# Order of a few small VectorE and GpSimd steps at the seams between attention units

## The reference

```
x: 8 batches x 512 tokens x 128 channels;  16 heads of 64;  all float32
h = layernorm(x) * (1 + ca) + sa
q, k, v = h @ Wq.T, h @ Wk.T, h @ Wv.T          # each cut into 16 heads
q = q / |q| * q_scale ;  k = k / |k| * k_scale  # per head and token
p = softmax(q k^T / 8)                          # per head, 512 x 512
x = x + ga * (concat(p v) @ Wo.T + bo)
h = layernorm(x) * (1 + cb) + sb
x = x + gb * (experts(h) + shared(h))           # top 2 of 8 experts, GELU
```

## Time and profile before

| what | value |
|---|---|
| median of 3 runs | 1392.53 us (1389.64 to 1394.34) |
| profiled execution | 1390.22 us, of which the span is 1388.5 us |
| PE busy | 1252.9 us, 90% of the span |
| DVE busy | 1059.7 us, 76% |
| ACT busy | 977.0 us, 70% |
| POOL busy | 860.8 us, 62% |
| granted clock, mean | 0.973 of full speed |

### The profile page before, as it was taken

How to read it: one execution, slowest core, us unless ns; L and a number is a source line. 1 busy time by engine, 2 the same in 40 slices (tenths; PEclk the granted TensorE clock), 3 DMA queues, 4 the chain that set the end, 5 groups by cost and what they waited for, 6 DMA issues and landing times. The chain is left out here.

```text
span 1388.5 us, 31896 instructions
## 1 busy us (share of the span) xinstructions
PE 1252.9 (90%) x9674; PEld 818.7 (59%) x9674; DVE 1059.7 (76%) x1947; ACT 977.0 (70%) x2078; POOL 860.8 (62%) x1675
## 2 busy tenths in 40 slices
PE   4799999999999999999999999999995477999997
PEld 4555655656555565656565555666553355777775
DVE  3778877868777787778787777877773995788887
ACT  3677767777767776777777677777763564777776
POOL 2577667766667776677666677766746674444443
PEclk8899999999999999999999999999998798999999
DMA  5000000000000000000000000000002001434341
GB/s 133 1 2 1 2 1 2 2 4 2 1 4 2 2 1 4 2 2 2 4 2 2 4 2 2 2 2 2 1 2 77 0 0 26 122 90 101 89 94 32
DMA packets 53201, 28.60 MB, mean 21 GB/s; under 512 B 8720, under 2 KB 51224, under 8 KB 53016
## 3 DMA queue, kind: packets, MB, share of 16 engines
q1 hardware_dynamic: 51832, 25.99, 7.8%
q10 hardware_dynamic: 1184, 0.40, 0.1%
HBM read 24.16 MB, written 2.23 MB: 19 GB/s over the span
## 5 line engine op out<-in xcount | busy, mean ns | idle before, releaser
L714 ACT ACTIVATE probs<-bank,neg_max 128x512 f32<-128x512 f32 x512 | 347.2, 683 | 249.4 <-DVE neg_max L836 238.5
L836 DVE TENSOR_REDUCE neg_max<-bank 128x1 f32<-128x512 f32 x512 | 329.3, 685 | 161.0 <-PE bank L533 157.8
L573 PE MATMUL bank<-probsT,qkv 128*64 128x512 f32 x1024 | 276.2, 619 | 0.9 <-DVE oT L853 0.9
L533 PE MATMUL bank<-operands 64*128 64x512 f32 x1536 | 249.8, 430 | 1.4 <-ACT probs L714 0.9
L1003 POOL TENSOR_TENSOR inv_wide<-inv_sum,consts 128x512 f32<-128x512 f32 x64 | 66.5, 1039 | 220.9 <-DVE inv_sum L847 220.9
L549 PEld LDWEIGHTS T<-ident,probs 64*128 64x128 f32 x4096 | 170.0, 139 | 42.5 <-issue 14.7
L549 PE MATMUL T<-ident,probs 64*128 64x64 f32 x4096 | 171.1, 223 | 2.6 <-issue 1.4
L503 PEld LDWEIGHTS bank<-operands,hT_h 128*128 128x128 f32 x254 | 47.8, 188 | 209.7 <-issue 206.3
L1637 POOL TENSOR_TENSOR hid_l<-gated,hid_h 128x512 fp32r<-128x512 f32 x64 | 88.9, 1389 | 125.4 <-ACT hid_h L1554 125.4
L533 PEld LDWEIGHTS bank<-operands 64*128 64x128 f32 x1536 | 125.7, 186 | 63.3 <-issue 41.7
L842 DVE COPY probsT<-T 128x1024 f32<-128x1024 f32 x128 | 155.6, 1215 | 0.2
(11 more groups left out here) (237 smaller groups left out, 2379.2 us busy)
## 6 DMA issues: line engine op xcount, KB each, us to landing
probsT<-gate_scratch SPq DMA_DIRECT2D x64, 256.0 KB, 4.9
out<-x_all SPq DMA_DIRECT2D x8, 256.0 KB, 2.3
probsT<-in_L_ffn_fc_w SPq DMA_DIRECT2D x1, 1024.0 KB, 9.8
raw<-in_L_attn_Wq SPq DMA_DIRECT2D x1, 512.0 KB, 4.4
raw<-in_L_attn_Wk SPq DMA_DIRECT2D x1, 512.0 KB, 7.3
raw<-in_L_attn_Wv SPq DMA_DIRECT2D x1, 512.0 KB, 8.4
raw_o<-in_L_attn_Wo SPq DMA_DIRECT2D x1, 512.0 KB, 8.6
probsT<-in_L_ffn_sh_w SPq DMA_DIRECT2D x2, 256.0 KB, 2.7
```

The costliest lines, as they stand in the source:

```text
L533: last = nc.tensor.matmul(s_bank(hp, 2 * pair + head)[:], own[rows, q, toks], own[rows, k], start=((q, k) == (QH, KH)), stop=(q == QL))
L573: last = nc.tensor.matmul(O_BANK[rows, :], qkv[:, hp % 4, j, cols], probsT[:, hp % 2, head, j], start=(j == 0), stop=(j == NT - 1), skip_g ...
L714: nc.scalar.activation(probs[:, i % 4], s_bank(hp, i)[:], ACT.Exp, bias=neg_max[:, i:i + 1], accum_out=row_sum[:, hp % 2, i:i + 1]).then_i ...
L836: nc.vector.reduce_max(neg_max[:, i:i + 1], s_bank(hp, i)[:], AX.X, negate=True).then_inc(max_done, 1)
```

## The change

Two orders change, and no operation is added or removed.

On VectorE, in pair 0 of every slot, invert_sums(u-1) stands ahead of sum_squares(u+1) and guess_norms(u+1) instead of behind them. On GpSimd, in norm units, all four tiles of squares stand ahead of split_o(u-2); in the other units split_o stays between the first and the second tile.

```diff
@@ VectorE, slot
                             if pair == 2 and earlier >= 2:
                                 normalise(u - 2, hp - 2)
+                            if pair == 0 and earlier >= 1:
+                                invert_sums(u - 1, hp - 1)
                             if main and pair == 0 and with_next(b, hp, 1):
                                 sum_squares(u + 1)
                                 guess_norms(u + 1)
-                            if pair == 0 and earlier >= 1:
-                                invert_sums(u - 1, hp - 1)
@@ GpSimd, slot
                             square_projection(u + 2, hp + 2, 0)
-                        if earlier >= 2:
+                        split_late = main and norm_of(b, hp)
+                        if earlier >= 2 and not split_late:
                             split_o(u - 2, hp - 2)
                         if main and with_next(b, hp, 2):
                             for t in range(1, NT):
                                 square_projection(u + 2, hp + 2, t)
+                        if earlier >= 2 and split_late:
+                            split_o(u - 2, hp - 2)
```

## The result

The changed kernel takes 1360.16 us (median of four runs, 1358.57 to 1361.32) against 1393.01 us before; the ratio is 0.9767, with a 95% interval from 0.9747 to 0.9787. The gain is 32.9 us where 24 were forecast, and the time lies 0.8 us under the low end of the range. The direction and the places were right, the size was not.

A forecast was written before the change was run, and what follows sets the result against it. TensorE's waits in attention, behind the norm units, were taken as the bound. Seams and unit 3 in batches 1 to 6 (20.7 us), last batch 1.8, short slots 1.5: 24.0 us, bounds 21 and 31; median 1368.5 us, range 1361 to 1384.

The forecast's parts named there:

- the chain: Behind norm units: late GpSimd squares, then VectorE's sum and guess, inversion, widen, refinement; 1.75 us lost in unit 1, 3.03 in unit 4.
- the 5.25 us: Units 1 and 4: TensorE's third pair starts 5.25 us after the refinement, so an earlier refinement brings that pair forward.
- the entry wait of 0.40 us: Unit 3: VectorE stands 0.40 us for the last exponential before the inversion, which now goes ahead of the sum.
- the sum that starts 0.6 us later in unit 3: VectorE in unit 3: with the wait and the inversion ahead of it, the sum of squares is 0.60 us late.
- The rival on the slower side: Every slot: widen stretches the sum by up to 1.0 us, giving 1417 us; chance 0.06.
- the guess waits for widen: Seams at units 1 and 4: guess operations wait for a begun widen's end; the last starts 0.33 us after it.
- the shift from unit 3: Before unit 4: unit 3's refinement comes 0.49 us sooner, and layer norm's guess, inverse_std and squares come that much sooner.
- unit 3 loses 0.1 us: Unit 3: first exponential released at 465.03 against scores at 464.96, a loss of 0.1 us a batch.
- 4 x 0.3: Batch 0: second pairs wait less for the earlier refinement, up to 0.37 us, taken as 0.3 for each of four units.
- entry wait in every ordinary unit: Rival: 0.40 us comes through in 5 units of 8 batches, 16 us back, 1384.5 us; chance 0.12.
- blocked more than once: Rival: each of the guess's three operations may lose a turn to GpSimd, half the gain lost, 1380.5 us; chance 0.08.
- no change: Rival: the seams' wait passes to another engine and the refinement was not what counted, 1391 us; chance 0.04.

The follow-up runs named there:

- GpSimd's part alone: Against the kernel before, only GpSimd's new order: squares ahead of split_o in norm units, VectorE still sums first and inverts afterwards; 1371.16 us, ratio 0.9848.
- VectorE's part alone: Against the kernel before, only VectorE's new order: inversion ahead of the sum of squares, GpSimd keeps its old order in norm units; 1367.47 us, ratio 0.9824.
- widen kept back: Changed kernel with one wait more: widen starts only after the guess of the same slot, so not beside the sum; 1387.64 us, ratio 0.9966.
- the kernel with the short split_o: Against the kernel with statistics behind the maxima: split_o of norm units makes the low part for only 128 of 512 columns; 1358.08 us, ratio 0.9763.
- The second measurement: The changed kernel run again, unaltered, beside the kernel before on one chip; 1363.51 us, ratio 0.9778.

## Why the prediction was wrong

**What held.** The bound (TensorE's waits in two units of eight), the chain, the 5.25 us (in unit 4; 5.36 in unit 1), the entry wait of 0.40 us, and the sum that starts 0.6 us later in unit 3 (0.79 us ahead of the scores before, 0.18 after). What failed are sizes of terms in the sum, above all the refinement at unit 4 (forecast 2.70 us after the first scores, measured 2.23), and a term for TensorE's clock, which the sum doesn't have. They follow one by one. In unit 3 after, the inversion and the sum start as follows (VectorE's timeline), against the earlier trace rows:

```profile
449.97 0.20 DVE L847 RECIPROCAL inv_sum<-row_sum 128x8 f32<-128x8 f32 x1 [0.32 <-ACT probs L714]
450.17 1.22 DVE L813 TENSOR_REDUCE ss<-sq 128x16 f32<-128x1024 f32 x1
```

The wait is 0.32 us of idle time, as in the earlier trace rows. The sum beside widen was taken as unblocked, and it was: over all 64 units L813 takes 1.184 to 1.222 us after and 1.203 to 1.223 before. The rival on the slower side, and with it a stretched sum, is refuted. The Trainium skill gives tensor_reduce only the 1x mode, in "VectorE: DVE Perf Modes", "The perf-mode tier table (the rule you actually need)", as the prediction had it; these lengths, the same beside GpSimd and alone, agree.

**Step "the guess waits for widen" was oversized.** It added the whole 0.33 us from the sum's end to the last guess operation behind widen's end. But an operation that is blocked has already begun and ends with GpSimd's: L818 ended 0.04 us after widen, and the last guess operation started at 467.28, 0.15 us after it. That is 0.2 us too much at each seam. The step from there to the refinement, estimated at 0.27 us from no row of its own, took 0.25 (467.53 - 467.28). The prediction also put 0.1 us between split_o's end and widen at unit 4, where there is none (464.85 + 1.28 = 466.13, widen at 466.10). At unit 1 widen ended at 421.98 (420.94 + 1.04) and L818, at 421.83, was not held up at all:

```profile
420.94 1.04 POOL L1003 TENSOR_TENSOR inv_wide<-inv_sum,consts 128x512 f32<-128x512 f32 x1
...
421.83 0.18 DVE L818 TENSOR_SCALAR ss<-ss 128x16 f32<-128x16 f32 x1
```

**Step "the shift from unit 3" was undersized.** The squares of unit 3 start 465.30 - 461.45 = 3.85 us ahead of unit 4's first scores. Before, the first tile started 0.57 us ahead of split_o, at 472.82, 3.18 us ahead. The shift is 0.67 us, not 0.49. About half of it is TensorE being later itself: unit 3 is longer by 0.31 us, and what GpSimd does meanwhile is not. The other half is the layer norm's guess, no longer held up: 0.34 us. In unit 4 of batch 3 the refinement starts 2.23 us after the first scores where the prediction had 2.70, and the 0.47 us are 0.2 from the guess, 0.1 from the gap ahead of widen and 0.18 from the shift. In unit 1 it starts at 2.01 us where 2.27 stood, of which pair 2 takes 0.15; the rest is that batch 3, which the prediction read, had a shorter unit 1 than the mean (17.14 and 17.23 us). Unit 4 thus gains 2.68 us where 2.2 were forecast and unit 1 gains 1.61 where 1.35 were, 0.74 us a batch, 4.4 us in all.

**Step "unit 3 loses 0.1 us" looked at one bank only.** It compared the first exponential with the scores of pair 1 and stopped. The loss is 0.31 us, most of it in the third pair: VectorE's statistics stand between the delayed copy and the maxima of pair 1, so ScalarE's exponentials are late, and behind them its copy of the T bank, for which TensorE's transposes wait. The third pair of unit 3 takes 3.99 us, 3.67 before. ScalarE and TensorE in unit 3 of batch 3:

```profile
457.77 1.02 ACT L719 ACTIVATE probsT<-T 128x1024 f32<-128x1024 f32 x1
...
458.89 0.71 PE L549 MATMUL T<-ident,probs 64*128 64x64 f32 x16 [0.20 <-issue]
```

The copy ends at 458.79, the transposes start at 458.89. The statistics moved behind the maxima take this loss away (14.61 us), which shows that it comes through them; that ScalarE's copy is the last link is read from these rows. Against what the prediction feared of such waits, though, the net effect of the entry wait in units 3 and 4 is a gain: without it the two take 30.45 us, with it 30.07.

**A term was missing: unit 5.** It gains 0.22 us. GpSimd's squares are over sooner, so VectorE's split of the normalised rows is held up less in pair 3. In batch 3, after:

```profile
491.57 0.50 DVE L865 CAST hT_h<-h_out 128x128 fp32r<-128x128 f32 x1
492.11 0.29 DVE L867 TENSOR_TENSOR hT_l<-h_out,hT_h 128x128 fp32r<-128x128 f32 x1
```

and before:

```profile
504.91 0.42 DVE L865 CAST hT_h<-h_out 128x128 fp32r<-128x128 f32 x1
505.36 0.60 DVE L867 TENSOR_TENSOR hT_l<-h_out,hT_h 128x128 fp32r<-128x128 f32 x1
```

With the old order in unit 5 it is back at 15.71 us, so the gain belongs to the inversion's place. That the held-up split is the way is read from these rows; it was not tried alone.

**Batch 0 and TensorE's clock.** Batch 0 gave 2.2 us where 4 x 0.3 stood. Its units 2 to 4 lose their whole 0.37 us of waiting. Unit 1 falls from 15.55 to 13.92 us, and the clock has a part in it. Before, TensorE stood 1.77 us for q and was then granted 0.79 of full speed, a mix of its two levels, 1.2 and 2.4 GHz; after, it stands 0.88 us and keeps full speed. That wait before and then after:

```profile
59.67 0.66 PE L512 MATMUL bank<-ident,qkv 128*128 128x128 f32 x4 [1.77 <-POOL qkv L997]
```

```profile
60.33 0.65 PE L512 MATMUL bank<-ident,qkv 128*128 128x128 f32 x4 [0.88 <-POOL qkv L997]
```

Stretches of the two kernels, before and then after (busy us and instructions of PE, PEld, DVE, ACT, POOL, then PEclk, the granted clock):

```profile
38.00:42.00 4.00, 2.69 (x12) 1.43 (x13) 3.91 (x10) 1.44 (x4) 1.20 (x6) 0.75 0.03 6
...
58.00:66.00 8.00, 6.33 (x43) 3.97 (x45) 3.08 (x4) 5.29 (x13) 4.59 (x8) 0.79 0.01 2
```

```profile
38.00:42.00 4.00, 3.21 (x12) 1.80 (x11) 3.81 (x10) 1.47 (x4) 1.31 (x6) 0.50 0.03 6
...
58.00:66.00 8.00, 7.12 (x82) 4.89 (x80) 4.79 (x7) 6.39 (x15) 5.25 (x10) 1.00 0.01 2
```

With GpSimd's part alone the stretch from 58 us is at 0.79 again and pair 2 of unit 1 takes 5.10 us, as before; with VectorE's part alone it is at 1.00 and 3.66 us. In all ten profiles the two go together: the clock fell there in the three with a wait of 1.77 to 1.81 us (before, GpSimd's part alone, widen kept back) and in none of the seven with 0.88 to 0.90. So halving the wait most likely kept the clock up, worth 1.4 us in one pair. Unit 0 goes the other way (14.15 to 15.17 us): at the start of attention the clock stayed at 0.50 after and rose to full speed sooner before, in slot 0, where the change moves nothing; the kernel with the short split_o rose sooner too (14.11 us). That is where the executions differ and is no effect of the change. The prediction had neither.

**The range.** Its low end, a gain of 31 us, allowed 7 us beyond the forecast, all of it for unblocked guesses. The attention part of the profiled pair came to 30.4 us, inside the bounds of 21 and 31; the other 2.5 us up to the measured 32.9 are scatter between executions, for which the range had no room: the kernel before alone spreads over 5 us, and its slower executions are those with the lower mean clock. The second measurement, 28.8 us by medians, would have lain inside the range; that the first lay 0.8 us outside it is in part bad luck. The terms above were too small all the same. The rival "entry wait in every ordinary unit" is refuted by units 2 and 6, unchanged within 0.01 us; "blocked more than once" by L39 and L40, 0.17 us each everywhere; "no change" by the waits.

## What to carry to other kernels

When two engines take turns on a chain, look for the step that needs neither the other's last result nor its data, and put it first: here it let 1.0 us of GpSimd's work run beside 1.2 us of VectorE's, and the pace followed wherever this chain was the last to end. Where two operations hold each other up, ask first which queue the next step stands in: here it stood behind widen anyway, so about half of what the blocked guess seemed to cost was widen's own place in time. A wait moved to the head of a queue has to be followed through every bank behind it, not only the first; and a unit that gets longer gives engines off the path a head start into the next one. Keep room in the range for single executions, not only for unknown prices, and compare the mean granted clock before comparing times that differ by a few us.

## What the runs showed of the hardware

- A small VectorE operation of the guess (TENSOR_SCALAR, 4 or 16 numbers per partition) that meets a GpSimd operation stands until that one's end and ends 0.03 to 0.04 us behind it: 1.00 us beside widen with the inversion first only behind norm units, 0.65 beside the low part with GpSimd's part alone, 0.39 in the changed kernel, 0.17 to 0.18 when free. As a rule one operation of a guess is held up, in the changed kernel never more. Not every small operation is: the inversion (RECIPROCAL, 8 numbers) took 0.20 us at 465.31, in the midst of split_o's low part (464.85 to 466.13). The Trainium skill says that two-port VectorE instructions and GpSimd's block each other ("Advanced Engine Details and Errata", "VectorE Performance Modes"); the runs add how long and which operations here.
- A reduction of 1024 numbers per partition from SBUF on VectorE runs beside GpSimd at full length: 1.22 us.
- The first pass of each loop edge costs TensorE about 2 us of idle time without a releaser in the profile (10.1 us in five times before, 10.6 after). Why it stands is open; it was not tried. That the edge's length varies is mostly the clock. Unit 7 of batch 2 took 17.46 us before and 19.27 after with the same instructions; before, the clock stayed at 1.00 behind it, after, it fell to 0.57 in the stretch from 402 to 406. In the ten profiles the 29 edges without a fall take 31.7 to 32.7 us (unit 7 and the next unit 0), the 21 with one 33.1 to 33.6, in the mean 1.3 us more. What decides whether it falls is not shown: the idle time was 1.83 us at one edge before where it fell and 2.13 at another where it didn't.

```profile
414.00:418.00 4.00, 3.82 (x33) 1.97 (x31) 3.21 (x8) 1.32 (x4) 2.69 (x9) 1.00 0.00 0
```

```profile
402.00:406.00 4.00, 3.55 (x9) 2.78 (x9) 1.61 (x4) 0.49 (x1) 2.73 (x9) 0.57 0.03 8
```
